# Choice of the kept tokens by counted ranks in place of a threshold search, with a second order for feed-forward and norm

## What is computed

```python
def _L0_ffn_ref(x, attention_mask, wr, br, w1, b1, w2, b2):
    b, s, d = x.shape                                    # 8, 1024, 64
    weights = (jnp.einsum('bsd,do->bso', x, wr) + br)[..., 0]
    k = max(1, int(CAPACITY * s)); kk = k - 1            # 512, 511
    _, idx = jax.lax.top_k(weights, k)
    sel_idx = idx[:, :kk]
    sel = ...                                            # those rows of x
    h = jax.nn.gelu(jnp.einsum('bkd,dh->bkh', sel, w1) + b1)
    y = jnp.einsum('bkh,hd->bkd', h, w2) + b2
    y = y * jnp.take_along_axis(weights, sel_idx, axis=1)[..., None]
    return jnp.zeros_like(x).at[jnp.arange(b)[:, None], sel_idx].set(y) + x
```

## Time and profile before

| | us |
|---|---|
| runs | 1122.30, 1123.24, 1123.25 (median 1123.24) |
| profiled execution, its own time | 1123.85 |
| its span | 1122.0 |
| start to first slot of the recurrence | about 35 |
| recurrence to its last step | to 808.2 |
| last tile, router, first unit | 808.2 to 826.2 |
| feed-forward, units 0 to 7 turned | 826.2 to 863 |
| second norm and phases | 863 to 901.2 |
| attention | 901.2 to about 975 |
| experts | to 1122 |

### The profile page before, as it was taken

One profiled execution on the slowest core, in us unless ns is written; L12 is line 12 of the kernel. 1 busy time (PEld: TensorE's weight loads), 2 busy tenths in 40 slices (PEclk: granted clock), 3 DMA queues, 4 the chain that ended last, 5 costly groups with the idle time before them and its releaser, 6 DMA issues.

```text
span 1122.0 us, 62678 instructions
## 1 busy us (share of the span) xinstructions
PE 1061.1 (95%) x26978; PEld 859.2 (77%) x26978; DVE 686.4 (61%) x3132; ACT 769.2 (69%) x4585; POOL 147.4 (13%) x220
## 2 busy tenths in 40 slices
PE   4799999999999999999999999999899879889998
PEld 2688899999999999999999999999744368833332
DVE  7566455555555555555555544444456758899996
ACT  1466677777767777777777776666567888667664
POOL 4300000011000100000110000000003402341320
PEclk9699999999999999999999999898699989999999
DMA  5000000000000000000000000000000000167786
GB/s 147 7 10 9 9 9 15 9 10 9 9 11 13 9 9 9 10 14 9 9 5 5 4 5 5 5 4 5 3 1 1 1 2 1 29 240 249 277 294 209
DMA packets 30642, 47.29 MB, mean 42 GB/s; under 512 B 12298, under 2 KB 21651, under 8 KB 30364
## 3 DMA queue, kind: packets, MB, share of 16 engines
q1 hardware_dynamic: 29820, 43.15, 11.5%
q10 hardware_dynamic: 544, 0.13, 0.1%
HBM read 40.88 MB, written 2.39 MB: 39 GB/s over the span
## 4 chain that ended last, share of the span: by engine, by line
PE 80%; DVE 9%; ACT 5%; issue 3%; DMA 2%; POOL 1%; SPq 0%; DVEq 0%; ACTq 0%; POOLq 0%
PE bank L680 44%; PE bank L777 7%; PE bank L671 5%; PE bank L760 4%; PE bank L441 3%; PE bank L540 2%; PE bank L1750 2%; PE bank L1696 2%; DMA space<-weights_kept 1%; PE bank L1437 1%; PE bank L1470 1%; PE bank L755 1%; DVE space L2159 1%; PE bank L1619 1%; PE bank L772 1%
## 5 line engine op out<-in xcount | busy, mean ns | idle before, releaser
L680 PE MATMUL bank<-space,whh_hi 128*128 128x32 f16 (+1 forms) x16384 | 574.0, 175 | 8.3 <-DVE space L808 4.4
L680 PEld LDWEIGHTS bank<-space,whh_hi 128*128 128x128 f16 x16384 | 481.9, 96 | 71.1 <-DVE space L808 8.0
L808 DVE TENSOR_TENSOR space<-h_f,space 128x16 f16<-128x16 f32 x2048 | 284.6, 176 | 365.5 <-ACT h_f L789 360.9
L789 ACT ACTIVATE h_f<-bank 128x16 f32<-128x16 f32 x2048 | 293.4, 184 | 226.4 <-PE bank L680 220.3
L795 ACT ACTIVATE space<-bank 128x16 f16<-128x16 f32 x2048 | 292.6, 184 | 1.1 <-PE bank L680 1.1
L671 PE MATMUL bank<-space,whh_lo 128*128 128x32 f16 (+1 forms) x2096 | 131.4, 177 | 0.0
L777 PE MATMUL bank<-space,wih_hi 128*128 128x32 f16 x2048 | 129.1, 177 | 0.0
L760 PE MATMUL bank<-xr,wih_hi 128*128 128x32 f16 x512 | 97.4, 190 | 0.0
L441 PE MATMUL bank<-onehot,tab 128*128 128x128 f16 x448 | 95.5, 219 | 0.5 <-DVE prepare_cur L491 0.5
L755 PE MATMUL bank<-ones,bias 128*128 128x32 bf16 x512 | 91.7, 179 | 0.0
L671 PEld LDWEIGHTS bank<-space,whh_lo 128*128 128x128 f16 x2096 | 90.1, 96 | 0.0
(11 more groups left out here) (309 smaller groups left out, 1598.9 us busy)
## 6 DMA issues: line engine op xcount, KB each, us to landing
space<-weights_kept SPq DMA_DIRECT2D x64, 512.0 KB, 7.8
space<-in_x SPq DMA_DIRECT2D x28, 129.0 KB, 3.1
out<-res SPq DMA_DIRECT2D x7, 256.0 KB, 9.8
space<-in_wrec SPq DMA_DIRECT2D x1, 768.0 KB, 4.3
space<-in_wx SPq DMA_DIRECT2D x1, 744.5 KB, 8.9
weights_kept<-wturned SPq DMA_DIRECT2D x8, 36.0 KB
whole<-weights_kept SPq DMA_DIRECT2D x8, 36.0 KB
brec<-in_brec SPq DMA_DIRECT2D x1, 260.0 KB
```

The source lines that it names most:

```text
L680: mm = pe.matmul(own[:, m, 0:copies, :], w[:, k, m * P:(m + 1) * P], state[:, k, :].unsqueeze(1).to_broadcast([P, copies, B]), start=False ...
L789: act.activation(h_f[layer][:, s % 2, :, :], own, ACT.Tanh, scale=scale[layer]).then_inc(s_h[layer], 1)
L808: dve.tensor_tensor(h[layer][:, :, s % RINGS[layer], 1, :], h_f[layer][:, s % 2, :, :], h[layer][:, :, s % RINGS[layer], 0, :], ALU.subtra ...
```

## The change

1. Ranks. A token is kept when few enough tokens beat it. For a pair of sequences, at the slots of its output, the router's two columns are turned into two rows on TensorE (`pair_turn`), copied by ScalarE (`pair_copy`), written to DRAM and read back to all partitions (`router_rows`, on SP's queue). VectorE compares each token's weight with the rows of all earlier tiles (`compare`, L622 of the changed kernel, 128 x 256 at a time) and with its own tile's (`compare_same`, L630; the constant `beyond` decides ties). A compare's accumulator gives how many beat the token; its 0/1 matrix `less`, summed over partitions by one-column matmuls (`rank_tensor`), gives what that tile adds to the ranks of earlier tokens. The sums are added into `limit`.
2. The compares of the last two pairs (`between`) and of the last tile (`compare_last`, `count_last`) come behind the recurrence. The digit search with its constants is gone, and the first turn (L1482) waits until the same-tile compares have read its banks.
3. Units run in the order 0, 4, 1, 5, 2, 6, 3, 7, so that a sequence pair is complete every second unit. The second norm of sequences 0 to 3 is put into the later units on all engines; the order of norm, phase and value work behind them is rewritten.
4. `rounded` of sequences 0 to 3 and `absolute` of 0 and 1 move from the attention to the end of the phase stage. POOL's eight copies of `candidate` become one (`one_row`), and one memset is added.

```diff
+        FIRST, SECOND = (101, 103, 108), (109, 110, 111)
+        def compare(dve, m, i, c):
...
+            dve.tensor_scalar(less[:, 3 * i + c, 0:count, :], first_rows[:, 2 * c:2 * c + count, b0 + i, :],
+                              wr[:, at:at + 1], 0.0, ALU.is_lt, ALU.add,
+                              accum_out=beaten[:, at, c:c + 1]).then_inc(s_less, 1)
+        def compare_same(dve, row, at, w, n):
...
+            dve.scalar_tensor_tensor(same[:, n % 2, :], row, w, beyond[:, :], ALU.subtract, ALU.is_lt,
+                                     accum_out=beaten[:, at, 3:4]).then_inc(s_less, 1)
+        def rank_vector(dve, m, o):
...
+            if o == 84:
...
+                dve.tensor_scalar(by_seq(wr[:, :])[:, b0:b0 + 2, j], by_seq(O_WR)[:, b0:b0 + 2, j], inv[:, S_WR:S_WR + 1],
...
+            elif o in FIRST + SECOND:
...
+                        dve.wait_ge(s_router_rows, 16 * (4 * j - 4 + m % 4 + 1))
...
+                    compare(dve, m, i, c)
+            elif o in (118, 120):
...
+                dve.wait_ge(s_router_rows, 16 * (m + 1))
...
+                dve.tensor_tensor(own, O_COUNT[:, :, 0:j], own, ALU.add).then_inc(s_taken, 1)
+        def pair_turn(pe, m):
...
+            pe.transpose(W_TURN, by_seq(wr[:, :])[:, b0:b0 + 2, j], eye[:, :]).then_inc(s_pair_turned, 1)
...
+        def pair_copy(act, m):
+            act.wait_ge(s_pair_turned, m + 1)
...
+            act.activation(wr_rows[:, :], W_TURN, ACT.Copy).then_inc(s_pair_kept, 1)
+        def rank_tensor(pe, m, o):
...
+            if o == 92:
+                pair_turn(pe, m)
...
+                for t in range(a, z):
+                    mm = pe.matmul(O_COUNT[:, i, t:t + 1], less[:, 3 * i + t // 2, t % 2, :], ones[:, 0:1], start=True,
...
+            if o + 2 * PERIOD == 93 and 0 <= k - 6 < SUBS:
+                pair_copy(act, k - 6)
...
+            rank_vector(dve, k - 6, o + 2 * PERIOD)
+            rank_vector(dve, k - 7, o + 3 * PERIOD)
+            rank_vector(dve, k - 8, o + 4 * PERIOD)
...
+        UNITS = (0, 4, 1, 5, 2, 6, 3, 7)
...
+            def router_rows(m):
...
+                sp.wait_ge(s_pair_kept, m + 1)
+                sp.dma_start(router_kept[j, b0:b0 + 2, :], wr_rows[:, :]).then_inc(s_router_out, 16)
+                sp.wait_ge(s_router_out, 16 * (m + 1))
...
+                sp.dma_start(rows_at(j)[:, b0:b0 + 2, :],
...
             recurrence(act, slot)
+            pair_copy(act, SUBS - 1)
             table(ACT.Gelu_apprx_tanh)
...
             ff_gelu(1, 1)
-            act.wait_ge(s_enough, 1)
-            act.activation(wall, banks[3][:, :], ACT.Copy).then_inc(s_kept, 1)
             ff_sum(0)
             ff_kept(0)
-            for b in range(1, B - 3):
-                ff_gelu(b + 1, 0)
-                ff_sum(b)
-                ff_gelu(b + 1, 1)
-                ff_kept(b)
-            for b in (B - 3,):
-                ff_gelu(b + 1, 0)
-                ff_sum(b)
-                ff_gelu(b + 1, 1)
-                second_square(0)
-                ff_kept(b)
-            ff_gelu(B - 1, 0)
-            ff_sum(B - 2)
-            second_square(1)
-            ff_gelu(B - 1, 1)
-            second_high(0)
-            ff_kept(B - 2)
+            for n in range(1, B):
+                if n < B - 1:
+                    ff_gelu(n + 1, 0)
+                ff_sum(n)
+                if n < B - 1:
+                    ff_gelu(n + 1, 1)
+                if n >= 2:
+                    second_square(n - 2)
+                if n >= 3:
+                    second_high(n - 3)
+                ff_kept(n)
+                if n >= 4:
+                    second_copy(n - 4)
             table(ACT.Gelu)
-            ff_sum(B - 1)
-            second_square(2)
-            second_copy(0)
-            ff_kept(B - 1)
-            second_high(1)
-            for b in range(1, B):
-                phase_gelu(b - 1)
-                if b > 1:
-                    second_high(b)
-                    phase_tanh(b - 2)
-                second_copy(b)
-                if b + 2 < B:
-                    second_square(b + 2)
-            phase_gelu(B - 1)
-            phase_tanh(B - 2)
-            phase_tanh(B - 1)
+            phase_gelu(0)
+            second_square(6)
+            second_copy(4)
+            second_high(5)
+            phase_gelu(1)
+            phase_tanh(0)
+            second_square(7)
+            second_copy(5)
+            phase_gelu(2)
+            phase_tanh(1)
+            second_high(6)
+            phase_gelu(3)
+            second_copy(6)
+            phase_tanh(2)
+            phase_gelu(4)
+            second_high(7)
+            phase_tanh(3)
+            phase_gelu(5)
+            second_copy(7)
+            phase_tanh(4)
+            phase_gelu(6)
+            phase_tanh(5)
+            phase_gelu(7)
+            phase_tanh(6)
+            phase_tanh(7)
             table(ACT.Sin)
...
-                    pe.wait_ge(s_kept, 1)
+                    pe.wait_ge(s_less, compared(SUBS) + 2 * AHEAD + B)
...
+            for n in range(B):
+                if 0 < n < B - 1:
+                    ff_hidden(n + 1, 0)
+                if n == 0:
+                    count_last(0)
+                elif n == 1:
+                    count_last(2)
+                    count_last(3)
+                elif n == 2:
+                    count_last(7)
+                ff_second(n, 0)
+                if n == 0:
+                    count_last(1)
+                elif n == 1:
+                    count_last(4)
+                ff_second(n, 1)
+                if 0 < n < B - 1:
+                    ff_hidden(n + 1, 1)
+                if n >= 4:
+                    pe.wait_ge(s_xt, OPEN + n - 4)
+                    stream(bank[5], 4)
+                    second_turn(n - 4)
+                ff_turned(n)
+                if n == 1:
+                    count_last(5)
+                    count_last(6)
+            turn_at = {0: 4, 1: 5, 2: 6, 4: 7}
             for b in range(B):
                 kq_hidden(b)
-                if b < B - 1:
-                    kq_values(b)
+                if b < 2:
+                    second_turn(turn_at[b])
                 kq_second(b, 0)
-                if 0 < b + 1 < B:
-                    second_turn(b + 1)
                 kq_second(b, 1)
+                if b in (2, 4):
+                    second_turn(turn_at[b])
+                if b != 1:
+                    kq_values(max(b - 1, 0))
             kq_values(B - 1)
...
+            def between():
+                rank_vector(dve, SUBS - 2, 118)
+                rank_vector(dve, SUBS - 2, 120)
+                rank_vector(dve, SUBS - 2, 139)
+                for o in FIRST + SECOND:
+                    rank_vector(dve, SUBS - 1, o)
+            halves_vector(dve, link, done, SUBS, begin, after, between,
...
+            rank_vector(dve, SUBS - 1, 139)
+            rank_vector(dve, SUBS - 1, 118)
+            rank_vector(dve, SUBS - 1, 120)
             dve.wait_ge(s_rw, SUBS + 2)
...
+            dve.tensor_scalar(w_last[:, :], by_seq(O_WR)[:, :, tile], inv[:, S_WR:S_WR + 1], column(WR_B), ALU.mult,
...
-            for r in range(8):
...
+            dve.tensor_copy(by_seq(wr[:, :])[:, :, tile], w_last[:, :])
+            def compare_last(b):
...
+                dve.tensor_scalar(less_last[:, b % 4, 0:6, :], first_rows[:, :, b, :], w, 0.0, ALU.is_lt, ALU.add,
+                                  accum_out=beaten[:, at, 0:1]).then_inc(s_less, 1)
+                dve.tensor_scalar(less_last[:, b % 4, 6, :], sixth_rows[:, b, :], w, 0.0, ALU.is_lt, ALU.add,
+                                  accum_out=beaten[:, at, 1:2]).then_inc(s_less, 1)
+            for b in range(AHEAD):
+                compare_last(b)
+            dve.wait_ge(s_wall, 1)
+            for b in range(B):
+                compare_same(dve, banks[3][:, b * P:(b + 1) * P], b * TT + tile, w_last[:, b:b + 1],
...
+            for b in range(AHEAD, B):
+                compare_last(b)
+            dve.wait_ge(s_less, compared(SUBS) + 3 * B)
...
+            values_at = {6: (0, 1), 7: (2,)}
...
-                    values_kept(b - 1)
+                for v in values_at.get(b, ()):
+                    values_kept(v)
+            dve.tensor_scalar(lnb[:, :], ones32[:, :], column(LN_B), None, ALU.mult).then_inc(s_lnb, 1)
+            rounded(0)
+            values_kept(3)
+            absolute(0)
+            rounded(1)
+            values_kept(4)
+            absolute(1)
+            values_kept(5)
+            rounded(2)
+            values_kept(6)
+            rounded(3)
             values_kept(B - 1)
```

311 lines of the change are left out of this document (163 added, 148 removed).

## The result

| | before | changed |
|---|---|---|
| executions, us | 1122.30 to 1123.25 (median 1122.98, 4) | 1139.52, 1138.95, 1133.43, 1138.64 (median 1138.8) |
| ratio | | 1.0127, 95% interval 1.0115 to 1.0139 |
| profiled execution, its own time and span | 1123.85, 1122.0 | 1139.52, 1137.7 |

A forecast was written before the change was run, and what follows sets the result against it. No engine is full behind the recurrence, so queue order was taken to set the time. Terms 1.0 + 5.7 + 5.7 + 1.1 - 2.7 - 1.4 - 1.0 = +8.4 us on 1123.24 gave 1131.6, range 1124.5 to 1139.

The forecast's parts named there:

- the first square: Behind the recurrence, ScalarE's table load waits for the last router pair's copy, so its first square comes 2.9 us later.
- the first scale: VectorE's first scale behind the recurrence, held by VectorE's own queue, comes 4.9 us later, at 819.8.
- the stop between square and high part: Feed-forward units 4 to 7: ScalarE idles 1.45 us before a high part whose scale VectorE queues behind a variance needing the square.
- VectorE's nine operations: Two same-tile compares, one addition and six compares ahead of the first scale take 3.9 us on VectorE.
- Recurrence: Slots of the recurrence: +1.0 us, all from count matmuls on TensorE; the compares fit VectorE's free 0.55 us.
- The counts' term: Count matmuls at 0.026 us each exceed the fuller slot's spare 0.06: 0.9 us, plus 0.1 in the other slot.
- To the first turn: From the recurrence's end to the first feed-forward turn (L1482): +5.7 us, 831.9 against 826.22.
- Part (c): Behind the last router weights, VectorE's 4.3 us of compares and 3.1 of same-tile ones hold the first turn's PSUM banks.
- Units: Feed-forward after the first turn: +5.7 us; turns 1 to 3 unchanged, units 4 to 7 take 6.1, 6.6, 6.6, 6.4.
- the terms +1.1, -2.7 and -1.4: +1.1 us to ScalarE's feed-forward end, -2.7 for the phase stage, -1.4 for a first sine no longer waiting for rounding.
- an overrun of the compares: Rival in the recurrence: compares overrun all 96 slots by 0.08 us, giving 1139.6; chance 0.10.
- The first rival: The overlap works: four ScalarE stops of 1.45 us vanish and value sums do not hold TensorE, 1120.8 us; chance 0.12.

The follow-up runs named there:

- e3: Changed kernel with the last two pairs' compares moved behind the last tile's router weights, their counts in another PSUM bank: 1138.92 us.
- e7: Changed kernel plus 18 filler matmuls in TensorE's idle stretch, and the last tile's router rows spread by matmuls over 64 rows instead of 8: 1135.36 us.
- e11: Changed kernel with table load first, gelu between, fillers, 64-row spread, counts six slots on, new phase order with 12 fillers, last values first: 1122.77 us, ratio 0.9995.
- e1: Changed kernel with the last router pair's copy moved behind ScalarE's table load, warm-up and register loads: 1136.14 us.
- e2: Changed kernel with one gelu of each feed-forward unit (kept rows in the last) between the second norm's square and high part on ScalarE: 1135.87 us.
- e6: Changed kernel with the last values kept ahead of the last of the four roundings on VectorE: 1134.22 us.
- e9: Changed kernel with each pair's first group of count matmuls moved six slots on, behind the reading of output sums sharing their PSUM bank: 1136.12 us.
- e10: Changed kernel with next hidden sums directly behind phase sums on TensorE, and VectorE keeping values one step earlier, in the phase stage: 1131.85 us.

## Why the prediction was right or wrong

- **Direction and most of the mechanism held.** The order of the queues cost time where it was said to. The three places named are in the profile: the first square comes 2.99 us later (2.9 forecast), the first scale 3.91 (4.9), and the stop between square and high part is 1.35 (1.45). Taking the first away brought the scale and, at equal clock, the first turn 1.9 earlier; taking the third away shortened the units by 3.0. For the second, VectorE's nine operations, e3 shows the scale 1.8 earlier and no gain in the end.
- **Recurrence, +1.0 forecast, +2.45 measured.** The compares fit their slots, as said: 0.47 us and a read within it, and no L924 came late behind one. The counts' term was mis-sized. I put the spare time of the full slot at 0.06 and charged only what exceeded it. But the pair of L540 takes 0.13 (503.90 to 504.03 in the earlier trace rows, 770.52 to 770.65 after), where I let it take 0.07, so there is no spare time at all. Slots with one to six counts grew by 0.02 to 0.15, about 1.8 in sum against 0.9, although only two of the four slots with six counts that I charged lie within the recurrence. The rest is single long slots, of which nothing was in my sum.
- **To the first turn, +5.7 forecast, +6.82 measured.** Two errors of opposite sign lie in this term. At full clock it is 21.85 - 18.02 = 3.8 (e7), all of it the scale's delay; the nine operations take 3.0 and not 3.9, since the compares cost 0.40 apiece, not 0.48, and the same-tile ones 0.27, not 0.38. Part (c) had the wrong path: I let the first turn wait for 7.4 us of compares on VectorE behind the router weights, but it waits for `yt` behind TensorE's spread and second sums, 3.3 us as before, and the compares end earlier. And the low clock, 3.0, isn't in the sum: I filled VectorE's wait with work and did not ask what TensorE does meanwhile. It stood idle, and its clock fell.
- **Units, +5.7 forecast, +7.03 measured.** 5.98, 6.45, 6.49 and 6.23 for the last four against 6.1, 6.6, 6.6, 6.4. For unit 4 the size came out by another cause: TensorE has no gap in it, so it is not ScalarE's stop that makes its 5.98. "Turns 1 to 3 keep 4.98" failed: the first step is 5.44 with full clock and 6.88 with half, and the next two are 9.86 against 9.42 before. Groups of seven counts stand on TensorE in these units; that they make the difference is argued from their length (0.33 us a group), not tried.
- **Last turn to first sine, -3.0 forecast** (the terms +1.1, -2.7 and -1.4), **+0.1 measured.** The first sine comes 16.4 later than before's, and 8 to 9 was the sign named for being right. 1.7 of the 3.1 is the clock near 883; without it the stage is 2.1 shorter than before against 1.6 forecast, and the load-to-sine piece is 2.0 longer than forecast. ScalarE's waits were 9.1 by my sheet and are 9.8 in its seven largest rows, so that held; but the first sine's wait did not go, it was turned into one for L1801, which needs the last values, which stood behind a rounding: 2.12 in place of 1.42 before. I said that the rounding is done and did not look at what else the change had put in its place.
- **Attention, -1.0 forecast, -0.7 measured.**
- **The sum without the clock:** 15.7 - 6.2 = 9.5 against 8.4. That is nearer than the terms deserve: the junction was forecast 1.9 too high (1.2 up to the router weights, 0.7 by a path that isn't there), the recurrence 1.5 and the sine 2.0 too low. The range held because its upper end had been set by another mechanism, an overrun of the compares, that did not occur; that is luck in part.
- **The first rival** (1120.8, the stops vanish and the values do not hold TensorE) describes e11 rather well, which needed e1, e2, e6, e7, e9, e10 and twelve more fillers to get there. As the kernel stands it did not happen.

## What to carry to other kernels

When work on one engine is lengthened, look at what TensorE does in that time: here a wait of 3.2 us was followed by a stretch at half clock, and matmuls without a result kept the clock up. They have to end before the next real input arrives: where they did not, the turn came 0.8 us later. An operation whose input comes from another engine in reply to the operation just ahead of it in the queue will wait the whole round; put something independent between them. Ask of each wait on a path also what else ends just before it: the work that I put on VectorE behind the router weights was no wait at all, since TensorE's own chain took longer. And a removed wait is only gone when everything that the next stage needs has been followed back, not just the operation that was last before.

## What the runs showed of the hardware that was not expected

- The granted clock fell twice more behind the recurrence in the changed kernel, and the phase of these falls differs from execution to execution: the medians of kernels that differ by one edit are blurred by 2 to 5 us, their stretches behind the recurrence at equal clock by 0.1.
- Of two kernels with about the same busy time of TensorE ahead of 830.6 (7.10 and 6.85 us of 7.60), the first had half the clock behind it and the second the full one; they differ in how many rows a stretch of matmuls there used, 8 or 64. The fall is in six of nine profiles with 8 rows and in none of four with 64, and it isn't settled.
- TensorE loses 0.2 to 1.1 us in single slots of the recurrence without a recorded wait, from none to nine times a kernel, at slots of which several recur in many of the kernels (near 276, 443, 459 and 587 us).
